# Second layer norm of a token sorter: statistics per token on the partitions, one product per token tile for turning, centring and routing

## The reference, cut to what matters

```
def _layernorm(x, axis=-1, eps=1e-05):
    m = jnp.mean(x, axis=axis, keepdims=True)
    v = jnp.var(x, axis=axis, keepdims=True)
    return (x - m) / jnp.sqrt(v + eps)
...
    x = _layernorm(x + _L1_attn_ref(x, ...), axis=-1)
    x = _layernorm(x + _L1_ffn_ref(x, ...), axis=-1)
```

## Time and profile before

| | us |
|---|---|
| median of 3 runs | 1781.83 (1779.89 to 1788.48) |
| the profiled execution, its own time | 1783.47 |
| its span in the profile | 1781.6 |
| PE busy in the span | 1567.7 (88%) |
| DVE busy | 1329.3 (75%) |
| ACT busy | 1274.3 (72%) |
| POOL busy | 522.3 (29%) |

### The profile page before, as it was taken

One profiled execution on the slowest core, in us unless ns is written; L12 is line 12 of the kernel. 1 busy time (PEld: TensorE's weight loads), 2 busy tenths in 40 slices (PEclk: granted clock), 3 DMA queues, 4 the chain that ended last, 5 costly groups with the idle time before them and its releaser, 6 DMA issues. The chain is left out here.

```text
span 1781.6 us, 39372 instructions
## 1 busy us (share of the span) xinstructions
PE 1567.7 (88%) x14020; PEld 850.5 (48%) x14020; DVE 1329.3 (75%) x1939; ACT 1274.3 (72%) x2407; POOL 522.3 (29%) x742
## 2 busy tenths in 40 slices
PE   5999999999979999999999999978999745476297
PEld 4555555555543444344444444446777312134287
DVE  2777777777769999999999999737555358756375
ACT  2777777777745989889898998966888478113187
POOL 0222222222244000110100013037889114123366
PEclk8999999999986999999999999989999866786599
DMA  2121100100013010010001000023334000021221
GB/s 77 25 88 53 53 18 18 24 18 18 18 26 117 18 31 8 6 31 19 4 18 31 20 13 28 2 72 66 78 80 92 15 0 0 0 105 44 62 68 33
DMA packets 37595, 66.70 MB, mean 37 GB/s; under 512 B 9744, under 2 KB 17688, under 8 KB 36960
## 3 DMA queue, kind: packets, MB, share of 16 engines
q1 hardware_dynamic: 32096, 58.13, 13.2%
q0 software_dynamic: 5376, 6.96, 1.4%
HBM read 32.49 MB, written 6.09 MB: 22 GB/s over the span
## 5 line engine op out<-in xcount | busy, mean ns | idle before, releaser
L1000 ACT ACTIVATE m_probs<-m_ring 128x512 f32<-128x512 f32 x1024 | 542.6, 598 | 78.5 <-PE m_ring L916 62.7
L1079 DVE TENSOR_REDUCE m_half_max<-m_pairs 128x2 f32<-128x1024 f32 x512 | 587.8, 1212 | 12.8 <-PE m_pairs L899 12.4
L387 DVE TENSOR_REDUCE a_neg_max<-a_scores 128x1 f32<-128x1024 f32 x257 | 310.5, 1214 | 91.7 <-PE a_scores L314 91.6
L375 ACT ACTIVATE a_probs<-a_scores,a_neg_max 128x1024 f32<-128x1024 f32 x256 | 285.1, 1114 | 124.4 <-DVE a_neg_max L387 124.4
L931 PE MATMUL m_acc<-m_probs,m_v_aug 128*32 128x256 f32 (+1 forms) x4032 | 327.3, 397 | 0.0
L916 PE MATMUL m_ring<-m_q_max,m_k 32*128 32x512 f32 x1024 | 318.4, 499 | 4.0 <-DVE m_q_max L1093 3.0
L899 PE MATMUL m_pairs<-m_k,m_q 32*128 32x512 f32 x1024 | 264.0, 513 | 13.4 <-DVE m_half_max L1079 9.9
L314 PE MATMUL a_scores<-a_q,a_k_own 64*128 64x512 f32 x516 | 261.0, 622 | 6.5 <-ACT a_probs L375 5.6
L314 PE MATMUL a_scores<-a_q,a_k_other 64*128 64x512 f32 x516 | 259.4, 622 | 0.5
L916 PEld LDWEIGHTS m_ring<-m_q_max,m_k 32*128 32x128 f32 x1024 | 146.7, 183 | 217.9 <-ACT m_probs L1000 113.7
L422 POOL TENSOR_TENSOR a_scaled<-values,a_inv 128x128 f32<-128x128 f32 x256 | 102.1, 399 | 389.2 <-DVE a_inv L405 258.3
(11 more groups left out here) (287 smaller groups left out, 2168.3 us busy)
## 6 DMA issues: line engine op xcount, KB each, us to landing
e_gates<-sorted_results SPq DMA_DIRECT2D x64, 256.0 KB, 8.7
a_k_other<-a_k_own SPq DMA_DIRECT2D x66, 128.0 KB, 2.3
m_k<-m_k_init SPq DMA_DIRECT2D x8, 512.0 KB, 6.9
m_q<-xT SPq DMA_DIRECT2D x8, 512.0 KB, 7.3
f_records<-sorted_tokens SPq DMA_DIRECT2D x40, 68.0 KB, 1.8
e_w<-e_w_dram SPq DMA_DIRECT2D x1, 2064.0 KB, 7.7
xT<-x_t_dram SPq DMA_DIRECT2D x1, 2048.0 KB, 7.8
m_v_aug<-v_init_dram SPq DMA_DIRECT2D x1, 2048.0 KB
```

The source lines that it names most:

```text
L375: nc.scalar.activation(probs[:, g, :], scores[:, slot(h * G + g), :], ACT.Exp, bias=neg_max[:, g:g + 1], accum_out=total[:, g:g + 1]).then ...
L387: nc.vector.tensor_reduce(neg_max[:, i % G:i % G + 1], scores[:, slot(i), :], AX, ALU.max, negate=True).then_inc(max_done, 1)
L1000: nc.scalar.activation(probs[:, u % SLOTS, head, :], ring[:, bank, :], ACT.Exp, scale=0.5).then_inc(ring_taken, 1)
L1079: nc.vector.tensor_reduce(half_max[:, pair // PAIRS % 2, at:at + 2], pairs[:, pair % 2, :, :], AX, ALU.max).then_inc(pair_taken, 1)
```

## The change

The norm no longer works on chunks with channels on the partitions. DVE first makes the centring matrix C = I - 1/128 (`turn_w`, 128 columns). PE multiplies the router by it, and the 8 columns that result are copied behind C, so that `turn_w` has 136 columns. Then one product per token tile, with the tile of `xT` as the stationary operand and `turn_w` as the moving one, gives the tile turned (tokens on partitions), centred, and its centred logits in one go. The results stay in PSUM, three tiles in a bank, three banks for a batch and two sets of banks.

ACT takes the sum of squares of each token from PSUM, one ACTIVATE with `accum_out` per tile. The squares themselves go to one buffer, so each waits for the one before. One Ln and one Exp on 128x8 elements give the inverse deviation of a whole batch. ACT then copies each tile to `records` with that column as its scale: 3 tiles ahead of the Exp of the softmax, 5 behind it. DVE multiplies the logits of each bank by the inverse deviation (three small operations), adds the bias, and goes on with the unchanged chains `choose` and `put`, now simply batch after batch. POOL, SP and `table` are as before, save that POOL counts tiles in place of chunks.

```diff
@@ place_stage, tensors
-        mean = core.ps("p_mean", [D, 2, BANK], st)
-        var = core.ps("p_var", [D, 2, BANK], st)
-        turned = core.ps("p_turned", [TILE, 2, BANK], st)
-        logits = core.ps("p_logits", [TILE, BANK], st)
+        turned = core.ps("p_turned", [TILE, 2, BANKS, BANK], st)
@@ tensor (means, variances and the old turn are removed)
+                def turn(b):
+                    for t in range(b * PER_BATCH, (b + 1) * PER_BATCH):
+                        if b >= 2:
+                            pe.wait_ge(copied, in_bank_of(t) - 2 * PER_BATCH)
+                        nc.tensor.matmul(of_tile(t, 0, WIDTH), src[:, t * TILE:(t + 1) * TILE], turn_w[:, :], start=True,
+                                         stop=True).then_inc(turned_done, 1)
...
+                pe.wait_ge(centre_made, 1)
+                nc.tensor.matmul(ranks[:, 0, 0:E], turn_w[:, 0:D], router[:, 0:E], start=True, stop=True).then_inc(route_done, 1)
+                pe.wait_ge(route_copied, 1)
+                turn(0)
+                turn(1)
                 pe.wait_ge(order_in, 16)
+                for b in range(B):
+                    rank(b)
+                    if b + 2 < B:
+                        turn(b + 2)
@@ scalar
+                def square(t):
+                    act.wait_ge(turned_done, in_bank_of(t))
+                    if t:
+                        act.wait_ge(squared_done, t)
+                    b = t // PER_BATCH
+                    if b >= 2:
+                        act.wait_ge(log_done, b - 1)
+                    nc.scalar.activation(squared[:, :], of_tile(t, 0, D), ACT.Square,
+                                         accum_out=sums[:, b % 2, t % PER_BATCH:t % PER_BATCH + 1]).then_inc(squared_done, 1)
...
+                def scale(t):
+                    b = t // PER_BATCH
+                    act.wait_ge(scaled, b * BANKS + t % PER_BATCH // IN_BANK + 1)
+                    nc.scalar.activation(records[:, t, 0:D], of_tile(t, 0, D), ACT.Copy,
+                                         scale=inverse[:, b % 2, t % PER_BATCH:t % PER_BATCH + 1]).then_inc(copied, 1)
...
+                for b in range(B):
+                    tiles = range(b * PER_BATCH, (b + 1) * PER_BATCH)
+                    for t in tiles:
+                        square(t)
+                    invert(b)
+                    act.wait_ge(inverse_done, b + 1)
+                    for t in tiles[:FIRST]:
+                        scale(t)
+                    act.wait_ge(to_exp, b + 1)
+                    nc.scalar.activation(p[:, :, :], x[:, :, :], ACT.Exp).then_inc(exped, 1)
+                    for t in tiles[FIRST:]:
+                        scale(t)
@@ vector, choose (centre and the old scale are removed)
-                    dve.wait_ge(turned_done, BATCH_CHUNKS * (b + 1))
-                    nc.vector.tensor_tensor(x[:, :, :], logits[:, 0:PER_BATCH * E].rearrange("p (t e) -> p t e", e=E),
-                                            row(router[:, E:2 * E]), ALU.add).then_inc(biased, 1)
+                    dve.wait_ge(turned_done, (b + 1) * PER_BATCH)
+                    dve.wait_ge(inverse_done, b + 1)
+                    for bank in range(BANKS):
+                        n = min(IN_BANK, PER_BATCH - bank * IN_BANK)
+                        at = slice(bank * IN_BANK, bank * IN_BANK + n)
+                        of_bank = turned[:, b % 2, bank, 0:n * WIDTH].rearrange("p (t c) -> p t c", c=WIDTH)
+                        nc.vector.tensor_tensor(x[:, at, :], of_bank[:, :, D:], inverse[:, b % 2, at].unsqueeze(2)
+                                                .broadcast_to([TILE, n, E]), ALU.mult).then_inc(scaled, 1)
+                    dve.wait_ge(scaled, (b + 1) * BANKS)
+                    nc.vector.tensor_tensor(x[:, :, :], x[:, :, :], row(router[:, E:2 * E]), ALU.add).then_inc(biased, 1)
@@ vector, the stage's list
+                nc.vector.tensor_tensor(turn_w[:, 0:D], ident, mean_w, ALU.subtract).then_inc(centre_made, 1)
                 nc.vector.memset(eps[:, :], EPS).then_inc(eps_set, 1)
+                dve.wait_ge(route_done, 1)
+                nc.vector.tensor_copy(turn_w[:, D:], ranks[:, 0, 0:E]).then_inc(route_copied, 1)
...
+                for b in range(B):
+                    choose(b)
+                    put(b)
                 table()
```

More of the change, by code:

```diff
@@ L1843, with place_stage @@
 I32 = mybir.dt.int32
[L1846 removed]
+def place_stage(core, src, mean_w, ident, router, order, iota, records, scratch, tile_expert, tile_base, loads):
     nc = core.nc
[L1854 removed]
     PER_BATCH = TILES // B
[L1856 removed]
+    WIDTH = D + E
+    IN_BANK = 3
+    BANKS = -(-PER_BATCH // IN_BANK)
+    FIRST = 3
     before, resets = order[:, 0:D], order[:, D:D + E * PER_BATCH]
@@ new lines, in invert @@
+                def invert(b):
+                    act.wait_ge(squared_done, (b + 1) * PER_BATCH)
+                    nc.scalar.activation(log_var[:, b % 2, :], sums[:, b % 2, :], ACT.Ln, bias=eps[:, :],
+                                         scale=1.0 / D).then_inc(log_done, 1)
+                    act.wait_ge(log_done, b + 1)
+                    if b >= 2:
+                        act.wait_ge(biased, b - 1)
+                    nc.scalar.activation(inverse[:, b % 2, :], log_var[:, b % 2, :], ACT.Exp,
+                                         scale=-0.5).then_inc(inverse_done, 1)
```

116 lines of the change are left out of this document (21 added, 95 removed).

## The result

| | us, median (range, runs) |
|---|---|
| before | 1781.84 (1778.83 to 1793.60, 12) |
| changed | 1774.28 (1765.57 to 1778.92, 12) |
| ratio | 0.9941, 95% interval 0.9920 to 0.9961 |

The changed kernel is 0.6% faster: 7.6 us, where 21.3 were forecast. Its profiled execution took 1773.25 us with a span of 1771.2 (before: 1783.47 and 1781.6). The placing stage, the last but one of the program, runs from one ACT_TABLE_LOAD of ACT to the next in either trace. It is 83.4 us long before and 73.4 after, so the stage gives back 9.9 us and not 21.3.

What follows compares the result with a forecast made beforehand. No engine was full; a PE-DVE-ACT wait ring bound the placing stage. An earlier first softmax (8.7 us) and shorter periods (12.8), with POOL then unbroken, gave 21.3 us: 1783.47 - 21.3 = 1762.2, so 1762; range 1757 to 1769.

Steps and rivals of the forecast that it cites:

- The first softmax, 8.7 us earlier: Placing stage's start to the first bias addition: expected at 1597.0 against 1605.74, 8.7 us earlier.
- the two cases: PE's first products at full or half clock: first bias addition at 1596.7 or 1597.3; 1597.0 was taken.
- The period, 10.14: Time between batches' bias additions, DVE's choose, put and multiplications with ACT hidden: 10.14 us, 12.8 us less to the fourth slots.
- From the slots to the last scatter: Fourth batch's slots to POOL's last scatter start: 0.81 us, then seven steps in 8.93, untouched by the change.
- the rule against the change: VectorE and GpSimd exclude each other on SBUF, so denser DVE work could stretch scatters; each 0.1 us moves the end 3.2.
- POOL is the next to be late: Eight scatters at 1.276 take 10.2 us against the 10.14 period, so POOL's 31 steps run unbroken, 39.55 us.
- beside the last scatters: At the stage's end, SP's padding blocks follow the last put and stay hidden, adding no time.
- a wait that I took for met is not: Rival: a PE ordering wait or ACT's copies ahead of Exp add 2 us per period, 6 in all: 1768; chance 5%.

Runs made afterwards that it cites:

- e3: Changed kernel with all GpSimd scatters held until the fourth batch's slots are made; ratio 1.0038, stage 91.5 us.
- h3: Changed kernel with 2048-element GpSimd fills before batches two to four and every ScalarE square done twice; one execution, stage 70.7 us.
- k2: Changed kernel with 512-element GpSimd fills before batches two and three and eight square buffers; ratio 0.9882, stage 61.4 us.
- k4: Changed kernel with eight square buffers and one GpSimd fill, before the third batch only; one execution, stage 62.4 us.
- f1: Changed kernel with GpSimd waiting before batches two to four until the earlier batches' scatters have landed; ratio 0.992, stage 67.5 us.
- f2: Changed kernel with a 2048-element GpSimd fill (1.8 us) before the scatters of batches two to four; ratio 0.9918, stage 67.4 us.
- g1: Kernel before, old norm, with GpSimd's scatters held so that they run in two groups of 16; ratio 1.012, stage 97.8 us.
- e4: Changed kernel with 40 extra semaphore increments on DVE and SP and 20 on ACT at the stage's start; ratio 0.9936, stage 72.7 us.
- m1: Changed kernel with eight buffers for the squares and no fills; ratio 0.9931, stage 71.4 us.
- m2: Changed kernel with the fill's buffer allocated but never used, moving later SBUF addresses; ratio 0.9956, stage 72.5 us.
- h2: Changed kernel with 2048-element GpSimd fills before batches two and three only; ratio 0.9903, stage 65.4 us.
- h4: Changed kernel with 2048-element GpSimd fills before batches two and three and eight square buffers; ratio 0.9891, stage 64.1 us.
- k1: Changed kernel with 1024-element GpSimd fills before batches two and three and eight square buffers; ratio 0.9904, stage 62.4 us.
- h1: Changed kernel with all scatters held until the fourth slots and 24 GpSimd fills of 1216 elements run before them; one execution, stage 92.6 us.
- k3: Changed kernel with each scatter cut to 64 of 128 rows and 32 whole scatters added behind; one execution, stage 105.7 us.
- e2: Kernel before, unaltered, profiled again; one execution, 1782.12 us, stage 83.4 us.

## Why the forecast was off

By its own steps:

- **The first softmax, 8.7 us earlier: right.** The bias addition moved from 15.5 to 6.8 of the stage, 8.7. TensorE kept the full clock (granted 1.00, 2.4 GHz, from 1588.48 to 1595.26 in the first window), the better of the two cases. Eight squares stand 0.46 apart where 0.41 was forecast: the record of the square is 0.28 and of the read 0.19 as worked out, but the hand-over is longer than the 0.04. That the sum hit to 0.1 is in part luck: for the full clock it gave 1596.7, which is 6.5 of the stage, the squares took 0.4 more, and I had taken the middle of the two cases.
- **The period, 10.14: right** where nothing disturbs it: 10.09 and 10.08, and 10.0 to 10.1 for all three periods of e3. DVE sets it and ACT is covered with 3.2 us to spare (forecast 3.1, h3).
- **From the slots to the last scatter: right**, 9.87 us where 9.74 was forecast. The scatters' records didn't stretch, so the rule against the change took nothing here.
- **The failed step is "POOL is the next to be late"** with its conclusion that the batches then follow at POOL's rate and that "POOL has no idle time left". Its rate was right (1.26 us a step). What was taken for free is that scatters without idle time leave the other engines alone. In the changed kernel DVE, ACT and SP get slow starts beside them: 6.7 us in the third chain, and 5.1 at the end, where SP's padding writes, which the forecast has "beside the last scatters", take 16.0 in place of 8.5 and outlast them. 21.3 - 6.7 - 5.1 = 9.5, and the stage gave back 9.9.
- **The rivals.** The nearest by its size was "a wait that I took for met is not", 6 us, but the mechanism is none of them: I asked whether GpSimd would be slowed by its neighbours, and never whether its neighbours would be slowed by it.

That the stage can be as short as forecast is shown: it is 61.4 in k2 and 62.4 in k4, and the forecast's is 83.4 - 21.3 = 62.1. k2 has two fills (1.1 us in all) and 1.4 us from the square buffers beside it.

**What is shown and what stays open.** Shown: the loss is slow starts. Among the traces that miss records, the chains have them only with scatters beside them (e3), and with enough of these in a row (f1, f2 against the changed kernel). They come with the old norm too (g1), and they don't hang on the place in the lists (e4), the squares' buffers (m1) or the SBUF addresses (m2), each taken alone. Not shown is what the other runs seemed to say: that fills of 0.54 us are enough (h2, h4, k1, k2), that a busy GpSimd alone does nothing (h1), or that half scatters do nothing (k3). Each of these was traced with full records, and no trace with full records has slow starts, whatever its kernel.

Open is what in the chip makes them, and first of all whether they come without the recording. Their company with missing records, in the same kernel too (e2 against before, f2 against h3), makes the recording the first suspect. It isn't proved, since every timed execution here was recorded (each has its span and granted clock). The ratio of the changed kernel, 0.9941 or some 10.5 us by estimate, fits the stage's 9.9, so its timed executions had the loss as well. The Trainium skill (NOTIFIC — the notification-queue block, section The write path) says that this block, when its internal buffers fill, holds back the engine rather than lose a record. No run here shows whether that took place; what the traces show is that records are missing. The changed kernel traced with full records, or timed without recording, would settle most of it.

## What to carry to other kernels

When a change removes the idle time of an engine that issues DMAs, ask what that idle time did for the others, and look at every engine's starts in the trace after, not only at durations: here the durations on DVE and ACT hardly changed, and 11.8 us were lost between starts. Instructions that need only their own engine's last one, at an even spacing that is no instruction's duration, are the mark of it. Then ask whether the trace is whole before you build on it: if a DMA group has no landing time, semaphore records are missing, and such a trace should be compared only with others of its sort. Five kernels with fills seemed to show a cure here, and none had a partner of its own sort without fills.

## What the runs showed of the hardware

- Beside GpSimd's indirect scatters, 1.26 us apart, VectorE, ScalarE and SyncE started instructions late, VectorE 0.70 or 1.39 us apart instead of 0.26, for 10 to 13 us at a time. The last packet of a scatter still ended 1.9 us after its start. This stands only in traces that miss semaphore records, eleven of twenty; whether the recording makes it is open.
- An indirect scatter of 64 rows takes 0.90 us and one of 128 rows 0.97, at steps of 1.20 and 1.26: halving the rows saved GpSimd 0.06 us a step.
- An ACTIVATE with an accumulator on 128 elements costs 0.46 us where each waits for the one before, and 0.25 where none does.
- A one-input TENSOR_SCALAR on 64 f32 elements took 0.77 us in place of 0.20 beside a GpSimd fill; two-input operations on the same elements didn't change.
